# State-space block with a mixture of experts: the product of mean and deviation on ScalarE, the routing's tables in a PSUM bank, and the order of stages set anew

## The reference, cut to what matters

```python
h = _layernorm(x, axis=-1) * (1 + ca) + sa
x = x + ga * _L0_attn_ref(h, ...)      # a selective scan
h = _layernorm(x, axis=-1) * (1 + cb) + sb
x = x + gb * _L0_ffn_ref(h, Wg, We, be)   # 8 experts, top 2

# in _L0_attn_ref, state size 16, along the 1024 tokens
dt = softplus(einsum(dt_raw, W_dt) + b_dt)
A_bar = exp(dt[..., None] * A);  dB_u = (dt * u)[..., None] * B_sel
h[t] = A_bar[t] * h[t-1] + dB_u[t];  y = sum_n(h * C_sel) + u * D_param

# in _L0_ffn_ref
probs = softmax(x @ Wg);  top_vals, top_idx = top_k(probs, 2)
gates = top_vals / sum(top_vals)
out = sum over the two chosen experts of gate * (x @ We[e] + be[e])
```

## Time and profile before

| | |
|---|---|
| median of 3 runs | 1279.12 us (1279.1 to 1287.44) |
| the profiled execution's own time | 1282.32 us |
| its span, first to last instruction | 1280.4 us |
| mean granted clock of TensorE | 0.848 of full |
| first scan starts, last scan starts | 52.7 and 1152.0 us |

### The profile page before, as it was taken

One profiled execution on the slowest core, in us unless ns is written; L12 is line 12 of the kernel. 1 busy time (PEld: TensorE's weight loads), 2 busy tenths in 40 slices (PEclk: granted clock), 3 DMA queues, 4 the chain that ended last, 5 costly groups with the idle time before them and its releaser, 6 DMA issues. The chain is left out here.

```text
span 1280.4 us, 13483 instructions
## 1 busy us (share of the span) xinstructions
PE 965.2 (75%) x4232; PEld 604.6 (47%) x4232; DVE 1059.5 (83%) x793; ACT 707.2 (55%) x1348; POOL 1024.5 (80%) x512
## 2 busy tenths in 40 slices
PE   5334444588878897788878887789778896789798
PEld 4101112255554564355644655356445564467576
DVE  1399999999999999898999999999989999992100
ACT  5754567555765568465755667456755474333200
POOL 1476777599997999699978999699969999796253
PEclk9665655689888998798988998799879999899799
DMA  4606150636244451537155433436162624412121
GB/s 156 150 15 164 44 121 1 149 105 156 61 111 121 113 143 48 143 100 181 42 118 143 115 105 76 123 108 173 34 157 76 148 75 115 120 47 66 43 75 58
DMA packets 90536, 131.20 MB, mean 102 GB/s; under 512 B 13529, under 2 KB 73505, under 8 KB 90465
## 3 DMA queue, kind: packets, MB, share of 16 engines
q1 hardware_dynamic: 90464, 130.34, 39.2%
HBM read 54.50 MB, written 8.65 MB: 49 GB/s over the span
## 5 line engine op out<-in xcount | busy, mean ns | idle before, releaser
L845 POOL TENSOR_TENSOR h<-h,Cr 128x1024 f32<-128x1024 f32 x256 | 602.0, 2368 | 131.2 <-DVE h L735 131.0
L735 DVE TENSOR_TENSOR_SCAN h<-av,ps 128x1024 f32<-128x1024 f32 x256 | 585.0, 2285 | 18.3 <-DVE ps L728 0.9
L504 PE MATMUL ps<-xg,we 128*128 128x256 f32 x2048 | 514.7, 409 | 29.8 <-POOL xg L877 22.4
L504 PEld LDWEIGHTS ps<-xg,we 128*128 128x128 f32 x2048 | 412.2, 206 | 137.4 <-issue 44.8
L544 ACT ACTIVATE av<-dd,An 128x1024 f32<-128x1024 f32 x256 | 289.9, 1142 | 141.5 <-DVE h L735 134.2
L877 POOL TENSOR_TENSOR xg<-h2T,gbc 128x1024 f32<-128x1024 f32 x128 | 303.5, 2372 | 76.5 <-DMA gbc<-gates 35.3
L728 DVE TENSOR_TENSOR ps<-ps,dd 128x1024 f32<-128x1024 f32 x256 | 315.4, 1232 | 39.9 <-DMA dd<-src 14.1
L412 PE MATMUL ps<-h,gam 128*32 128x512 f32 x1024 | 165.1, 775 | 32.3 <-POOL h L845 17.6
L393 PE MATMUL ps<-S,sel 64*128 64x512 f32 x128 | 56.0, 523 | 65.0 <-DVE ps L728 64.1
L773 DVE TENSOR_TENSOR X<-ps,X 128x512 f32<-128x512 f32 x32 | 22.0, 688 | 99.3 <-PE ps L476 99.1
L598 ACT ACTIVATE Cr<-ps 128x512 f32<-128x512 f32 x64 | 37.9, 593 | 94.5 <-PE ps L453 63.2
(11 more groups left out here) (96 smaller groups left out, 861.8 us busy)
## 6 DMA issues: line engine op xcount, KB each, us to landing
dd<-src SPq DMA_DIRECT2D x512, 128.0 KB, 2.4
gbc<-gates SPq DMA_DIRECT2D x128, 256.0 KB, 3.5
X<-in_x SPq DMA_DIRECT2D x8, 1024.0 KB, 7.3
out<-X SPq DMA_DIRECT2D x32, 256.0 KB, 3.6
XN<-in_x SPq DMA_DIRECT2D x7, 1024.0 KB, 7.3
we<-in_We SPq DMA_DIRECT2D x2, 1024.0 KB, 8.5
XN<-in_x SPq DMA_DIRECT2D x2, 512.0 KB, 5.1
Cr<-in_wmod SPq DMA_DIRECT2D x1, 1024.0 KB, 5.2
```

Of the source, the lines that this page charges most:

```text
L504: e = pe.matmul(ps[:, FB, m * 256:(m + 1) * 256], we[:, hf, 2 * ep + e2, m * P:(m + 1) * P], xg[:, i % XG, e2, hf], start=(ep == e2 == m = ...
L735: dve.tensor_tensor_scan(h[:, u % HS], av[:, u % AS], wide(BP), 0.0, ALU.mult, ALU.add).then_inc(s_scan, 1)
L845: pool.tensor_tensor(h[:, u % HS], h[:, u % HS], Cr[:, q], ALU.mult).then_inc(s_ch, 1)
```

## The change

Three things are changed.

1. `rsb` moves from DVE to ACT: in place of one multiplication of 128 x 8, eight instructions of 128 x 1 with the deviation as scale, right behind `rstd`.
2. The routing's tables move. `soft` reads the logits in the bank MB where `lT` left them, so ACT's copy (line 605) is gone. The difference to the maximum goes to pe_t in SBUF, which `softe` overwrites in place. The one-hot tables are columns 256 to 511 of the same bank (`table`), the total of the two gates lies in it too, and each operation gets at most one tensor from SBUF. The number of DVE instructions in `soft` and `top` stays 17. The bank is released by the last instruction of `top`, where before ACT's copy released it; `gT` waits for that. The semaphore s_g is gone.
3. AT is new, and with it the order on every engine. In a block of the steady part (numbers of b and units as for the experts of sample 3):
   - DVE: `soft 3, top 3` stand after `mul 142` instead of after `scan 142`; `oX(2,3)` after `mul 144` instead of after `scan 143`; `S`, `corr`, `zs` and `zX` shift by at most one step.
   - ACT: `xh(0,5,k)` stood between the two halves of `xh(1,3,k)` and stands, two at a time, among `exp 131` to `exp 134`, ahead of `stat(1,3)`.
   - POOL: `dt(4,1,0)` ahead of `ch 132`, `dt(4,1,1)` ahead of `ch 135`, `dt(5,0,0)` ahead of `ch 148`, `dt(5,0,1)` ahead of `xg(3,1,1)`, each one step earlier or a little more; `gam 5` between `ch 141` and `ch 142` (before: `gam 4` after `ch 127`). In the prologue `gam 0` stands ahead of `dt(0,0,0)`, before it stood behind both.
   - PE: `gT` ahead of `xT(0,5,0,0)` (before: behind), `C` in pairs.
   - SP: `gw` ahead of `ddu(j=2)` (before: behind), `gr` right behind the first `gl` (before: behind `ldx`, after `gl(1,0)`), `ldx2` after `gl(2,1)` and `ddt(j=3)`, followed by `gl(2,2)` and `ddu(j=3)` (before: after `gl(1,0)`), each `out` a few steps later.

```diff
@@ -21,14 +21,14 @@
-AT = dict(exp=-1.21, mul=1.08, scan=1.53, ch=6.84, Bs=0.19, y=7.26, stat0=-5.28, stat0s=0.98, rstd0=3.61,
-          rsb0=1.59, xh0=11.0, xh0s=0.0, xT0=14.39, xT0h=1.94, xTs=3.73, rxT0=-0.6, wx=5.18, rwx=-0.33, S=0.3,
-          ldx=33.57, gam=38.49, dl0=20.77, dl1=35.27, dls=3.25, rdl=-0.37, corr=1.62, dt=7.73, C=25.76,
-          CS=2.56, Cc=2.97, rC=-0.32, ddt=36.17, ddts=1.47, ddu=36.38, ddus=1.74, zs=4.09, ldx2=32.55, z=3.84,
-          zX=1.16, zd=1.62, stat1=4.55, stat1s=0.63, rstd1=9.44, rsb1=0.73, xh1=9.97, xh1s=0.0, xh1g=1.34,
-          xT1=11.24, xT1h=0.62, xT1s=1.34, rxT1=-0.73, lg=13.33, rlg=0.11, lT=0.58, rlT=-0.25, soft=2.26,
-          softe=-1.82, top=2.7, gT=1.83, rgT=-0.99, gw=11.19, gr=34.34, xg=22.19, xgs=1.74, gl=-2.54, f=-2.35,
-          fE=0.24, o=2.15, oX=3.12, out=15.62, md1=-34.13, gates=-49.65, ga=-3.38)
+AT = dict(exp=0.38, mul=0.18, scan=1.03, ch=8.08, Bs=0.46, y=7.81, stat0=-2.56, stat0s=0.53, rstd0=1.51,
+          rsb0=0.0, xh0=3.33, xh0s=0.48, xT0=15.1, xT0h=1.17, xTs=2.97, rxT0=0.72, wx=4.84, rwx=0.48, S=-0.84,
+          ldx=33.57, gam=21.82, dl0=20.32, dl1=35.83, dls=3.4, rdl=0.78, corr=0.67, dt=7.36, C=26.08, CS=2.53,
+          Cc=1.11, rC=0.3, ddt=35.05, ddts=1.99, ddu=35.38, ddus=2.4, zs=4.03, ldx2=41.97, z=5.37, zX=-0.52,
+          zd=1.88, stat1=6.76, stat1s=0.35, rstd1=9.58, rsb1=0.3, xh1=11.02, xh1s=0.0, xh1g=1.89, xT1=11.29,
+          xT1h=0.53, xT1s=1.71, rxT1=0.61, lg=13.79, rlg=0.47, lT=0.48, soft=0.65, softe=0.9, top=0.97,
+          gT=1.28, rgT=0.32, gw=10.35, gr=25.47, xg=23.09, xgs=1.78, gl=-1.14, f=-3.12, fE=0.95, o=3.15,
+          oX=1.97, out=19.09, md1=-43.56, gates=-88.26, ga=-17.92)
 def before(b, t, put):
@@ -99,7 +99,6 @@
     put(s, "lg", b)
     put(s + AT["rlg"], "read", "lg", b)
     put(s + AT["lT"], "lT", b)
-    put(s + AT["lT"] + AT["rlT"], "read", "lT", b)
     put(s + AT["soft"], "soft", b)
     put(s + AT["soft"] + AT["softe"], "softe", b)
     put(s + AT["top"], "top", b)
@@ -229,12 +228,9 @@
         wgp = sb("wgp", [P, 2, 32])
         G64 = sb("G64", [BLK * E, P])
         eps = sb("eps", [P, 1])
-        ga_t = sb("ga_t", [P, 5, BLK, E])
-        gs = sb("gs", [P, 6, BLK])
+        pe_t, G = sb("pe_t", [P, BLK, E]), sb("G", [P, BLK, E])
+        gs = sb("gs", [P, 4, BLK])
         iw = sb("iw", [P, 1, E])
-        T = [ga_t[:, i] for i in range(5)]
-        V = [gs[:, i] for i in range(6)]
-        G = T[4]
         s_xa, s_x, s_wa, s_w, s_we = (sem(n) for n in ("s_xa", "s_x", "s_wa", "s_w", "s_we"))
         s_wm = [sem(f"s_wm{i}") for i in range(2)]
@@ -256,7 +252,7 @@
         s_dt, s_dtu = sem("s_dt"), sem("s_dtu")
         s_br, s_a, s_bm, s_scan, s_ch, s_y, s_z = (sem(n) for n in
                                                    ("s_br", "s_a", "s_bm", "s_scan", "s_ch", "s_y", "s_z"))
-        s_lg, s_lge, s_g = sem("s_lg"), sem("s_lge"), sem("s_g")
+        s_lg, s_lge = sem("s_lg"), sem("s_lge")
         s_zt, s_zr = sem("s_zt"), sem("s_zr")
         s_xg, s_f, s_fe = sem("s_xg"), sem("s_f"), sem("s_fe")
         s_am, s_v = sem("s_am"), sem("s_v")
@@ -277,6 +273,10 @@
         def emptied(eng, key):
             eng.wait_ge(s_m[bank.at[key]], bank.nth[key] + 1)
+
+        def table(b, i):
+
+            return mb(("lT", b))[:, 256 + 64 * i:320 + 64 * i].rearrange("p (k e) -> p k e", e=E)
         def release(instruction, key):
@@ -466,8 +466,8 @@
                     for i in range(2):
                         e = pe.transpose(bk[:, i * P:(i + 1) * P], lgT(s[1])[:, i * P:(i + 1) * P], identf[:])
                 elif s[0] == "gT":
-                    pe.wait_ge(s_g, s[1] + 1)
-                    e = pe.transpose(bk[0:BLK * E, 0:P], G.rearrange("p k e -> p (k e)"), identf[:])
+                    emptied(pe, ("lT", s[1]))
+                    e = pe.transpose(bk[0:BLK * E, 0:P], G[:].rearrange("p k e -> p (k e)"), identf[:])
                 elif s[0] == "o":
                     _, b, c = s
                     pe.wait_ge(s_fe, 4 * b + c + 1)
@@ -599,10 +599,6 @@
                 elif s[0] == "lg":
                     done(act, s)
                     release(act.activation(lgT(s[1]), mb(s)[:, 0:256], ACT.Copy), s)
-                elif s[0] == "lT":
-                    done(act, s)
-                    lg = mb(s)[:, 0:256].rearrange("p (i j r) -> p j i r", i=2, j=4)[:, :, :, 0:E]
-                    release(act.activation(T[3].rearrange("p (j i) e -> p j i e", j=4), lg, ACT.Copy), s)
                 elif s[0] == "gT":
                     b = s[1]
                     done(act, s)
@@ -661,10 +657,16 @@
                     act.activation(rs[:, w, 3], rs[:, w, 1], ACT.Ln, bias=eps[:], scale=1.0 / D).then_inc(s_ln[w], 1)
                     act.wait_ge(s_ln[w], b + 1)
                     act.activation(rs[:, w, 4], rs[:, w, 3], ACT.Exp, scale=-0.5).then_inc(s_rd[w], 1)
+                elif s[0] == "rsb":
+                    _, w, b = s
+                    act.wait_ge(s_rd[w], b + 1)
+                    for k in range(BLK):
+                        e = act.activation(rs[:, w, 5, k:k + 1], rs[:, w, 0, k:k + 1], ACT.Identity, scale=rs[:, w, 4, k:k + 1])
+                    e.then_inc(s_rs[w], 1)
                 elif s[0] == "softe":
                     b = s[1]
                     act.wait_ge(s_lg, b + 1)
-                    act.activation(T[1], T[0], ACT.Exp).then_inc(s_lge, 1)
+                    act.activation(pe_t[:], pe_t[:], ACT.Exp).then_inc(s_lge, 1)
         @block.vector
         def _(dve):
@@ -708,14 +710,15 @@
                 dve.tensor_tensor(Dga[:], md[:, 4:6], Dp[:].unsqueeze(2).to_broadcast([P, 2, NB]), ALU.mult).then_inc(s_md, 1)
                 dve.wait_ge(s_md, 2)
-            def bc(i):
-                return V[i].unsqueeze(2).to_broadcast([P, BLK, E])
-
-            def first(oh, tie, w):
-
-                link(dve.tensor_tensor(T[w], T[oh], iw[:].to_broadcast([P, BLK, E]), ALU.mult))
-                link(dve.tensor_reduce(V[tie], T[w], AX.X, ALU.max))
-                link(dve.tensor_tensor(T[oh], T[w], bc(tie), ALU.is_equal))
+            def bc(v):
+                return v.unsqueeze(2).to_broadcast([P, BLK, E])
+
+            def first(b, oh, tie):
+
+                o, w = table(b, oh), table(b, 3)
+                link(dve.tensor_tensor(w, o, iw[:].to_broadcast([P, BLK, E]), ALU.mult))
+                link(dve.tensor_reduce(tie, w, AX.X, ALU.max))
+                link(dve.tensor_tensor(o, w, bc(tie), ALU.is_equal))
             def times_b(u):
                 b, hf, q, j = unit(u)
@@ -735,11 +738,7 @@
                 dve.tensor_tensor_scan(h[:, u % HS], av[:, u % AS], wide(BP), 0.0, ALU.mult, ALU.add).then_inc(s_scan, 1)
             def beside_scan(s):
-                if s[0] == "rsb":
-                    _, w, b = s
-                    dve.wait_ge(s_rd[w], b + 1)
-                    dve.tensor_tensor(rs[:, w, 5], rs[:, w, 0], rs[:, w, 4], ALU.mult).then_inc(s_rs[w], 1)
-                elif s[0] == "S":
+                if s[0] == "S":
                     _, b, c = s
                     hi = S[96:P, b % 2, c * CH:(c + 1) * CH]
                     dve.wait_ge(s_hi, 2 * b + c + 1)
@@ -773,27 +772,31 @@
                     release(dve.tensor_tensor(x2, mb(("o", b, c)), x2, ALU.add), ("o", b, c))
                 elif s[0] == "soft":
                     b = s[1]
-                    emptied(dve, ("lT", b))
+                    done(dve, ("lT", b))
                     if b == 0:
                         dve.wait_ge(s_const, 5)
-                    link(dve.tensor_reduce(V[0], T[3], AX.X, ALU.max))
-                    link(dve.tensor_tensor(T[0], T[3], bc(0), ALU.subtract))
-                    dve.tensor_scalar(T[3], T[0], 0.0, None, ALU.is_equal).then_inc(s_lg, 1)
+                    lg = mb(("lT", b))[:, 0:256].rearrange("p (i j r) -> p j i r", i=2, j=4)[:, :, :, 0:E]
+                    top = gs[:, 0].rearrange("p (j i) -> p j i", i=2)
+                    link(dve.tensor_reduce(top, lg, AX.X, ALU.max))
+                    top = top.unsqueeze(3).to_broadcast([P, 4, 2, E])
+                    link(dve.tensor_tensor(pe_t[:].rearrange("p (j i) e -> p j i e", i=2), lg, top, ALU.subtract))
+                    dve.tensor_tensor(table(b, 1).rearrange("p (j i) e -> p j i e", i=2), lg, top, ALU.is_equal).then_inc(s_lg, 1)
                     dve.wait_ge(s_lg, b + 1)
                 elif s[0] == "top":
                     b = s[1]
-                    first(3, 1, 2)
+                    T, tie, second, total = [table(b, i) for i in range(4)], gs[:, 1], gs[:, 2], mb(("lT", b))[:, E:2 * E]
+                    first(b, 1, tie)
                     dve.wait_ge(s_lge, b + 1)
-                    link(dve.scalar_tensor_tensor(out=T[4], in0=T[3], scalar=-2.0, in1=T[1], op0=ALU.mult, op1=ALU.add))
-                    link(dve.tensor_reduce(V[2], T[4], AX.X, ALU.max))
-                    link(dve.tensor_tensor(T[0], T[4], bc(2), ALU.is_equal))
```

(17 more changed lines are left out.)

## The result

The changed kernel takes 1244.15 us (median of 4, 1240.06 to 1246.99) against 1279.11: the ratio is 0.9713, 95% interval 0.9661 to 0.9765. Its profiled execution took 1246.99 us, with a span of 1244.7; the forecast was 1238, range 1225 to 1262.

The account below looks back on a forecast made before the run. DVE was taken to set the pace, with tiny instructions waiting for POOL. Savings 23.7 + 20.7 + 2.4 + 1.2 = 48.0 us, 5.6 given back: 1239.9 from the profiled 1282.32, 1236.7 from the median; said 1238, range 1225 to 1262.

Parts of the forecast that it names:

- What bounds the kernel: Scan loop: DVE sets the 140.7 us block, POOL has 13 us slack; three tiny DVE instructions wait for POOL's current instruction.
- (1): `rsb` leaves DVE: the 14 L741 inside the scan loop come off the pace, saving 23.7 us.
- (2): `soft` reads logits in PSUM, table operations have at most one SBUF operand: 20.7 us freed, PSUM price taken as nothing.
- The rule on PSUM's fixed cost: Routing instructions reading PSUM: the skill's 120 against 58 cycles would cost 8.8 us more; the forecast took nothing.
- Rival C: Routing instructions: PSUM operands cost 65 ns more each, 8.8 us in all, giving 1247 us; chance 0.05.
- (3): ACT takes `rsb` as eight instructions, 2.0 us, hidden in the loop; start gains 2.4 us, end 1.2.
- (4): Bank MB held from `lT` to the end of `top`: cost nothing, covered by `f(3,3)` on PE; 4.4 us of PE without cover.
- (5): Stages moved: ldx2 ahead of ddu(j=3) costs 0.8 us a block, 5.6 in seven; bounds no stall to 2.5 us.
- Rival B: ldx2 and a `gl` waiting for POOL delay ddu(j=3) all block; 5.9 us a block cancels the gain, up to 1301; chance 0.08.
- Rival A: POOL sets the pace or its lag delays `dt`, `zs` and output: blocks stay at 137.5 us, time 1260; chance 0.20.
- D: POOL also holds up small operations with one PSUM operand; only (1), start and end remain: 1257 us; chance 0.04.
- E: New order also removes DVE's 8.7 us output transpose wait: 1228 us; lower edge of the forecast's 0.60, no separate chance.

Follow-up runs that it names:

- `ldx2` early: Changed kernel with ldx2 right behind the last out of the sample two earlier, ahead of ddt(j=0); nothing else moved: 1237.5 us, ratio 0.9644 to the kernel before.
- its neighbour: Changed kernel with both ldx2 and out at the places they had in the kernel before: 1236.73 us, ratio 0.9647 to the kernel before.
- half the products: Changed kernel with ldx2 placed early and POOL's product with C on the first 512 columns only: 1235.42 us, ratio 0.9618 to the kernel before.

## Why the prediction was right, step by step

**What bounds the kernel.** Right. DVE's time set the block, and that its three tiny instructions waited for POOL was shown from both sides: by a shorter instruction on POOL, and by the tables put back into SBUF. One piece of the evidence was read wrongly. L716, at 226 ns at most, was taken as free of the wait beside POOL; its tensors lie in SBUF too, and it was short because POOL stood idle at all sixteen of them.

**(1) and (2), 44.4 us off the pace.** DVE's busy time fell by 45.0, where 25.3 and 20.7 make 46.0; the 8 ns more of PSUM to PSUM explain part of the rest. (The 1010 us that the last part of the prediction gives did not follow from its own terms, which give 1013.5; measured were 1014.5.) What the working did not have is that these waits are not fixed to an instruction. It counted each part by its own rows, and the expectations for the parts alone, 24 and 17 us, came from the same rows. They gave 11 and 10, and 34 together. That the parts could be added up was not worked out, and it was luck in so far as both were in the change, so that no instruction was left to take over the wait.

**The rule on PSUM's fixed cost.** By the row, nothing; by "VectorE: DVE Perf Modes" of the Trainium skill, section on the TRN2 errata, an estimate of about 65 ns for each of 17 instructions (16 of them read PSUM). Measured: 0 to 8 ns. Rival C is out.

**(3) ACT.** Eight instructions take 1.59 us (18.07 to 19.66 in the prologue), taken at 2.0. The scan waited for av nowhere in the six blocks. The start gained 2.8 us for 2.4. The end was to gain 1.2 and lost 0.2. `soft` of the last sample came 1.4 us earlier after the last scan (39.3 instead of 40.7), but `gT` then waited on PE behind `f(6,3,3)`. PE in order of time, in the changed kernel:

```profile
1155.25 5.31 PE L504 MATMUL ps<-xg,we 128*128 128x256 f32 x16
1160.49 1.13 PE L509 MATMUL ps<-rows,wrow 8*128 8x256 f32 x4
1161.54 0.30 PE L470 MATMUL ps<-identf,G 128*64 128x128 f32 x1
```

The same 16 matmuls took 3.62 us before. The granted clock tells why, in stretches over these matmuls, after and before (the last columns are granted clock, DMA share, GB/s):

```profile
1155.25:1160.50 5.25, 5.25 (x19) 4.05 (x17) 3.80 (x17) 0.26 (x1) 0.00 (x0) 0.67 0.01 3
```
```profile
1192.26:1195.80 3.54, 3.54 (x18) 2.85 (x16) 2.67 (x13) 0.48 (x2) 0.00 (x0) 1.00 0.01 2
```

A mean of 0.67 means that part of the stretch ran at 1.2 GHz, where before all of it ran at 2.4. In both kernels the same instructions stood ahead of it, with PE idle 1.25 and 0.6 us between them; why the clock fell in the one is not shown. `top` was done at 1159.80, PE took up `gT` at 1161.54: 1.7 us. The second profile of the changed kernel has the same 5.30 us there, and of all twelve profiles six have it and six have 3.62: `ldx2` early has it, its neighbour has not. So it comes again, and it hangs on more than the change.

**(4) The bank.** "Cost: nothing" fits what the new order shows and was wrong as a statement on the bank: in the order of before the same hold costs 8.5 us at the output transpose with the tables alone, and some 4 with both edits. What was missed is the step behind `gT`: `xT(0)` and `o` need the bank too. The new order moves `oX(2,3)` behind a multiplication and has 7.0 and 9.1 us of this wait in six blocks in its two profiles, 8.7 before.

**(5) `ldx2` ahead of ddu(j=3).** The place and the mechanism were right, the size was not: 0.8 us a block taken, 2.0 measured in the first profile, near the 2.5 that the working had as its upper bound, and 1.2 in the second. This is the main term that was mis-sized. It and 0.4 us a block for `lT`, which is not ready when DVE comes to `soft` (2.5 us in six), make 1.6 us a block more than forecast. A little more busy time saved, a shorter wait for the output transpose and smaller gaps bring that down to some 0.8, and so the loop gained 33.1 and not 38.8 us. The end gave 1.4 us less than forecast and the start 0.4 more. Rival B was thus true in kind, but stayed at a third of the 5.9 us a block that it needed to cancel the gain.

**POOL.** Its waits for the scan were to fall to 25 us in six blocks and fell to 22.9. Rival A did not happen. Its waits for gates rose from 14.7 to 28.5 us, without price as far as the runs show: with half the products it waits far longer and the time is the same.

**The rivals D and E.** D (small instructions wait even with an operand in PSUM) is out by the groups. E was to take away all of DVE's wait for the output transpose; it took 1.7 of 8.7 us in the first profile and nothing in the second (9.1).

## What to carry to other kernels

An instruction of 8 columns that takes 1.6 us in the mean and whose shortest is 0.16 is waiting while it counts as busy; compare its end with the other engines' ends, and ask whether all that it reads lies in SBUF. An instruction of the same kind that stays short is no proof against it before you have looked at what the other engine does at that time. Such a wait moves to the next instruction of its kind when it is taken from one, so take it from all of them together, and don't add up what each shows. And when an engine gets faster, look at the transfer with the least to spare before its need (here 2.7 us): a 1 MB load placed ahead of it cost 9.5 us of a change that won 35.

## What had not been expected of the hardware

The wait for POOL shows up at whichever instruction of this kind comes first while POOL is at work: L722 went from 224 to 614 ns in the mean when only `rsb` was removed, and `rsb` from 1583 to 1698 when only the tables were moved. And it can last longer than one instruction of POOL. The L741 of the earlier trace rows, from 756.33 to 760.23, stood beside two, this one and the product of the earlier trace rows from 757.76 to 760.20:

```profile
755.45 2.46 POOL L877 TENSOR_TENSOR xg<-h2T,gbc 128x1024 f32<-128x1024 f32 x1
```

Had it waited for the first alone, it would have ended near 757.9. Four of the sixteen took 3.8 us or more.

Four copies of 128 KB issued right behind a 1 MB load and a 256 KB one let DVE go on 6.8 us after their issue, instead of 2.4 from issue to landing.
